# Queue order of a self-attention step on TensorE: both score pairs, then the maxima products, then the weighted values

## The reference, cut to what matters

```python
qkv = (_ln(x, g_attn, b_attn) @ qkv_w + qkv_b)       # 16 heads of 16 columns
scores = einsum("bhqd,bhkd->bhqk", q, k) / sqrt(16)
scores = where(causal, -inf, scores)                 # sequence of 1024, batch of 2
attn = einsum("bhqk,bhkd->bhqd", softmax(scores), v)
```

## Time and profile before

| | |
|---|---|
| median of 3 executions | 1081.88 us (1072.76 to 1084.87) |
| the profiled execution | 1063.34 us |
| its span, first to last instruction | 1061.8 us |
| TensorE busy, mean granted clock | 902.9 us (85%), 0.924 |
| VectorE / ScalarE busy | 628.5 us / 465.3 us |
| first scores of quad 0 / quad 7 | 135.18 us / 356.14 us |

### The profile page before, as it was taken

How to read it: one execution, slowest core, us unless ns; L and a number is a source line. 1 busy time by engine, 2 the same in 40 slices (tenths; PEclk the granted TensorE clock), 3 DMA queues, 4 the chain that set the end, 5 groups by cost and what they waited for, 6 DMA issues and landing times. The chain is left out here.

```text
span 1061.8 us, 12280 instructions
## 1 busy us (share of the span) xinstructions
PE 902.9 (85%) x3899; PEld 546.5 (51%) x3912; DVE 628.5 (59%) x927; ACT 465.3 (44%) x683; POOL 170.5 (16%) x200
## 2 busy tenths in 40 slices
PE   5776599999999967999988899945663899999996
PEld 3553255555555424444446688622221477777774
DVE  4635667777777216377785544433331767777775
ACT  2311056565666734666655355313451343333332
POOL 7910012221222213000021300300110001111110
PEclk9897789999999988999998899966886989999999
DMA  3056534433353116000000000055773000000002
GB/s 122 13 200 173 211 88 110 101 81 85 88 130 92 42 59 257 1 0 1 0 1 25 0 1 1 22 189 166 198 198 118 16 1 20 21 20 20 20 20 79
DMA packets 34325, 79.30 MB, mean 75 GB/s; under 512 B 8120, under 2 KB 11192, under 8 KB 33896
## 3 DMA queue, kind: packets, MB, share of 16 engines
q1 hardware_dynamic: 29288, 70.64, 22.5%
q10 hardware_dynamic: 2688, 5.33, 1.4%
q0 software_dynamic: 2304, 2.76, 1.1%
HBM read 48.34 MB, written 30.10 MB: 74 GB/s over the span
## 5 line engine op out<-in xcount | busy, mean ns | idle before, releaser
L1049 DVE TENSOR_REDUCE part_max<-psum 128x4 f32<-128x512 f32 x288 | 185.9, 686 | 78.9 <-PE psum L1393 47.0
L757 ACT ACTIVATE prob<-psum 128x1024 f32<-128x1024 f32 (+1 forms) x192 | 145.2, 809 | 90.9 <-PE psum L1421 90.4
L1393 PE MATMUL psum<-k,q 128*128 128x512 f32 x288 | 121.8, 467 | 21.4 <-DMA k<-k 16.6
L1421 PE MATMUL psum<-q,k 128*128 128x512 f32 (+3 forms) x384 | 96.6, 358 | 11.8 <-ACTq L744 10.7
L1393 PEld LDWEIGHTS psum<-k,q 128*128 128x128 f32 x288 | 52.7, 196 | 84.6 <-DVE part_max L1049 53.8
L914 ACT ACTIVATE silu<-psum,wt 128x512 f32<-128x512 f32 x64 | 40.5, 685 | 116.8 <-DVE decide L1291 85.4
L651 POOL TENSOR_SCALAR_AFFINE_SELECT prob<-prob 128x256 f32<-128x256 f32 x128 | 52.7, 421 | 238.7 <-ACT prob L757 237.3
L1439 PE MATMUL psum<-prob,vq 128*32 128x512 f32 (+3 forms) x768 | 81.8, 498 | 2.2 <-POOL prob L651 1.3
L1421 PEld LDWEIGHTS psum<-q,k 128*128 128x128 f32 x384 | 66.1, 191 | 33.0 <-issue 11.4
L1302 DVE TENSOR_TENSOR masked_lo<-masked,masked_hi 128x1024 fp32r<-128x1024 f32 x32 | 46.5, 1454 | 38.6 <-ACT masked_hi L922 38.6
L327 PE MATMUL psum<-masked_hi,wt_hi 128*128 128x512 f32 x128 | 55.5, 434 | 6.4 <-DVE res L1307 6.1
(11 more groups left out here) (165 smaller groups left out, 1616.7 us busy)
## 6 DMA issues: line engine op xcount, KB each, us to landing
q<-q SPq DMA_DIRECT2D x8, 768.0 KB, 6.5
k<-k SPq DMA_DIRECT2D x16, 384.0 KB, 8.1
xq<-xq SPq DMA_DIRECT2D x8, 768.0 KB, 5.8
wt<-in_wt SPq DMA_DIRECT2D x8, 513.0 KB, 3.6
q<-part_hi SPq DMA_DIRECT2D x16, 256.0 KB
k<-part_hi SPq DMA_DIRECT2D x16, 256.0 KB
o<-stage SPq DMA_DIRECT2D x8, 512.0 KB, 7.2
xq<-xpart_hi SPq DMA_DIRECT2D x16, 256.0 KB
```

The source lines that it names most:

```text
L757: act.activation(A.prob[0:A.keys, s % 2, p, :, q0:CH], psum[0:A.keys, 2 * p:2 * p + 2, q0:CH], ACT.Exp, scale=SCALE)\
L1049: dve.tensor_reduce(part_max[:].rearrange("q (j p i) k -> q p j i k", j=2, p=2)[:, :, :, i, kt], heads, AX_X, ALU.max).then_inc(A.s1_free, 1)
L1393: mm = pe.matmul(heads, A.q1[:, qd, i * P:(i + 1) * P], A.k1[:, qd, :, k0:k0 + P], start=True, stop=not diag)
L1421: mm = pe.matmul(psum[0:A.keys, 2 * p + j, q0:CH], A.k2[:, qd, p, j, kt * P:kt * P + A.keys], A.q2[:, qd, p, c * CH + q0:(c + 1) * CH], st ...
```

## The change

For the causal attention alone, `scores(.., 1)` moves ahead of share 0, and shares 2 and 3 move ahead of `weigh`. A step was: scores 0, share 0, scores 1, share 1, weigh, shares 2 and 3. It becomes: scores 0, scores 1, shares 0 to 3, weigh. The instructions and their waits are the same, and so are the orders on all other engines; nothing changes in the cross-attention.

```diff
                         scores(it, qd, s, 0)
                         if s == 0 and not A.causal and more and not (isinstance(n, int) and n == 0):
                             turn(*after(it, qd, 1))
-                        ahead(it, qd, A.share(s, 0), more)
+                        if not A.causal:
+                            ahead(it, qd, A.share(s, 0), more)
                         scores(it, qd, s, 1)
+                        if A.causal:
+                            ahead(it, qd, A.share(s, 0), more)
                         ahead(it, qd, A.share(s, 1), more)
+                        if A.causal:
+                            ahead(it, qd, A.share(s, 2) + A.share(s, 3), more)
                         if s > 0:
                             weigh(it, qd, s - 1)
                         elif not (isinstance(n, int) and n == 0):
                             weigh(*after(it, qd, -1), A.nsteps - 1)
-                        ahead(it, qd, A.share(s, 2) + A.share(s, 3), more)
+                        if not A.causal:
+                            ahead(it, qd, A.share(s, 2) + A.share(s, 3), more)
```

## The result

| | before | after |
|---|---|---|
| median of 17 executions, same chips | 1075.37 us (1067.54 to 1085.56) | 1087.12 us (1080.68 to 1099.11) |
| ratio to before, 95% interval | | 1.0101 [1.0066, 1.0136] |
| first scores of quad 0 to first scores of quad 7, in the trace | 220.96 us | 234.11 us |

The changed kernel is slower by 1.0%, or some 11 us; the trace shows 13.15 us more in the changed stage. Forecast were 12.6 us and 1094 us, in a range of 1078 to 1108. The absolute figure is 7 us high mostly because the three executions of before that I started from had a higher median than 17 have.

What follows compares the result with a forecast made beforehand. TensorE, its queue full, bounds the self-attention. Added less removed waits gave 8.2 us for quads 1 to 5, 1.6 for quad 0 and 2.8 for quad 6: 12.6 on a median of 1081.9, so 1094 us, range 1078 to 1108.

Steps and rivals of the forecast that it cites:

- TensorE is full, so an order can only remove or add waits: Mid self-attention, TensorE busy 49.4 and 48.8 of 50 us; reordering removes no work, only removes or adds waits.
- The burst of four against three banks: Steps 0, 4, 6, 7: fourth unit waits 1.17 us from first's start; costs 0.35 each, 0.58 in step 7.
- Three-unit bursts cost nothing: Steps 1, 5 and 9 have three units and no wait, as the previous burst's maxima are over by then.
- A score pair behind weigh costs 0.10 more: After weigh now stands a score pair instead of a unit; the same 0.10 us extra was assumed for it.
- The transpose: Step 8: transpose waits 0.81 us for gather, formerly hidden by weigh; with unit 1' the step costs 0.93.
- The negation: Unit 2' no longer waits for the negation, since weigh 7 stands ahead of it; saves 0.80 us per quad.
- The masks: Weigh of step 0 no longer waits for GpSimd's masks; saves 0.13 us, with 0.2 to spare.
- Quad 6: Bursts cost 1.63 us; transpose right behind 35* waits 1.63 against 0.31 before; less 0.13, 2.8 us in all.
- Quad 0: First step has a lower clock and no weigh before it; the same 1.6 us loss was assumed.
- not slower: Rival: a bank is free within 0.7 us, so the fourth unit doesn't wait; 1076 us, chance 0.05.
- VectorE becomes the bound: Rival: in the burst, backlog carries from step to step and three-unit bursts wait too; 16 to 23 us, chance 0.15.
- Loads during the wait: Weight loads begin only with the waiting unit's product, per a trace row; loading during waits would make the sum 9.1 us.

Runs made afterwards that it cites:

- Experiment 1: Kernel before with only the second score pair moved ahead of share 0: 1070.98 us, ratio 0.9976 [0.9936, 1.0016].
- Experiments 4 to 7: Two banks instead of three: before 229.7 us over seven quads, changed kernel 268.0; maxima over half the keys: quad 3 31.17 us before, changed kernel 31.97.
- Experiment 3: Changed kernel with the transpose behind weigh in step 8: seven quads 230.7 us, ratio to before 1.011 [1.0069, 1.0151].
- The second profile: Changed kernel run once more, nothing altered: quads 1 to 6 took 33.55, 33.45, 33.46, 33.47, 33.47 and 31.70 us, quad 0 35.22.
- experiments 2 and 8: 2: kernel before with only shares 2 and 3 moved ahead of weigh, ratio 1.0006 [0.9962, 1.005], seven quads 224.3 us. 8: see experiment 8.
- 6 and 10: 6: kernel before with maxima over half the keys, quads 2 to 5 31.20, 31.17, 31.41 and 31.20 us. 10: see experiment 10.
- experiment 10: Changed kernel with only the fourth unit of steps 0, 4, 6, 7 and 8 (in 8 with the transpose) behind weigh: seven quads 221.1 us.
- experiment 8: Kernel before with weigh ahead of unit 2' in step 9: 1067.93 us, ratio 0.9952 [0.9912, 0.9991], seven quads 217.9 us.
- experiment 7: Changed kernel with each maximum taken over half the keys: quads 2 to 5 31.97 us each.
- experiments 8 and 9: 9: experiment 8 with VectorE's inversion of the sums four units later, ratio to before 0.9923 [0.9874, 0.9972], seven quads 217.2 us.

## Why the prediction was right, point by point

- **TensorE is full, so an order can only remove or add waits.** Right. Experiment 1 gives the cleanest proof: the score pairs moved, and no step of quad 3 changed by over 0.02.
- **The burst of four against three banks**: forecast 0.35 in steps 0, 4 and 6 and 0.58 in step 7, measured 0.35, 0.36, 0.36 and 0.61. The chain of 1.17 us (result 0.39, start of VectorE 0.04, maximum 0.69, back 0.05) was measured as 1.18. Experiments 4 to 7 and 10 turn its parts (banks, the maximum's time, the burst's length), and the loss follows.
- **Three-unit bursts cost nothing**: right; step 5 unchanged, step 1 and 2 together -0.13.
- **A score pair behind weigh costs 0.10 more**, as taken over from units: measured, the second score follows after 0.34 there instead of 0.23 (271.82 to 272.15).
- **The transpose**: forecast +0.93, measured +1.02. It began 2.32 after the burst's first unit (272.85 to 275.17), as forecast. Experiment 3 moves it away and step 8 falls by 0.88.
- **The negation**: forecast -0.80, measured -0.88; the wait is gone from the list. The surplus in both is where the records put the border between steps 8 and 9.
- **The masks**: forecast -0.13, measured -0.13 over steps 1 and 2. The spare time was less than the 0.2 I gave: before, weigh began 0.13 after the masks' end, so 0.13 of the time between them is no slack; in the changed kernel it began 0.23 after it (253.92 to 254.15), which leaves 0.1.
- **Quad 6**: forecast 2.8, measured 2.97. **Quad 0**: forecast 1.6, measured 1.65, and that is luck: step 0 lost nothing of the 0.35 of its burst, and step 1 lost 0.33 with the later rise of the clock. The second profile has 1.86. **Quad 7**: no change, 24.9 and 25.0 us to its last weigh.
- **The sum**: 12.6 forecast, 13.15 in the trace. Between the medians are 11.75 us (1087.12 - 1075.37). That the effect would be at the edge of 1% was right as well: the interval, 0.66 to 1.36%, holds 1%, so the executions show that the kernel is slower but not that it is slower by over 1%, on which I had put 0.58.
- **The rivals**: "not slower" needed a bank free within 0.7 us and got 1.18. "VectorE becomes the bound" didn't occur: in the changed order it reached the inversion of the sums after the DMA in quads 2 and 6 and 0.1 us ahead of it in quad 4, so there was nothing to pile up. It did occur, in a small way, behind the inversion in quads 2 and 4 of experiments 2 and 8 and in quad 4 of 6 and 10.
- **Loads during the wait**: the row was the right guide. The Trainium skill, TensorE: Matmul & The Clock Gate, Step-by-step: what each phase is for, says that the queue pulls weight loads ahead of matmuls in flight. The traces here agree within scores and units (the load at 277.01 ran beside the scores, 0.17 ahead of its unit), but no load went ahead of its own unit's wait: 270.38 in the changed kernel, 241.37 with halved maxima. Nor did one go ahead of a weigh: in experiment 10 the fourth unit's bank had been free since 248.02, and its load still began with its product at 248.91. So a wait isn't the only thing that stops the loads; why weigh does is open.

## What to carry to other kernels

Where a full engine feeds a slower consumer through n buffers, its instructions should be spread so that no more than n of them come within one round trip (here three within 1.2 us); grouping like with like saves nothing if the engine is already dense. A wait is best covered by putting other long work directly ahead of the waiting instruction, and the thing to check then is whether the consumer also waits for a DMA, whose landing need not come earlier when the steps get shorter. Compare starts step by step: busy shares stayed at 95% and more with 5% lost.

## What the runs showed that I had not expected

- The sums' DMA doesn't keep step with the queue. VectorE could go on about 17.0 us into quad 2 and 16.8 into quad 4 before, and at 17.5 and 17.8 in experiment 8, while it reached the inversion at 16.5 in both. A wait of 0.3 to 0.5 us there was free; waits of 1.0 and 1.3 us cost TensorE 0.4 and 0.7 us, over half of the gain of quad 2 and all of quad 4's. Why the DMA landed later in experiment 8 wasn't looked into.
- A wait that ends exactly in time still costs 0.09 to 0.10 us on TensorE, by the weight load behind it (experiment 7).
- Quad 0 takes 33.4 us before and not 31.7 because it begins at the lower clock level, and how long that lasts differs from trace to trace (2.9 to 5.9 us), also between the two of the changed kernel (5.35 and 5.9). That is why it gained 0.6 and 0.3 us in experiments 8 and 9, though its step 9 fell by 0.86 in both.
